# Self attention with ALiBi in a decoder layer: the place of the row sums' transposes, of the head maxima and of the output copy in each head, and norm scales computed on GpSimd

## What is computed

```python
x = _layernorm(x + _L0_attn_ref(x, ...))       # rotary q, k; alibi = min(j - i, 0) * slope * 8; no mask
x = _layernorm(x + _L0_xattn_ref(x, ctx, ...)) # cross attention on 1601 context rows
x = _layernorm(x + _L0_ffn_ref(x, ...))        # 8 experts, the best 2 of each row
# attention: w = softmax(q @ k.T * SCALE + alibi); out = w @ v;  _layernorm: (x - m) / sqrt(v + 1e-5)
```

## Time and profile before

| | us |
|---|---|
| median of 3 executions | 1904.31 (1903.47 to 1906.08) |
| the profiled execution | 1906.57 |
| its span | 1904.8 |
| PE busy | 1745.0 (92%) |
| DVE busy | 1390.0 (73%) |
| ACT busy | 1174.9 (62%) |
| POOL busy | 355.5 (19%) |

### The profile page before, as it was taken

One profiled execution on the slowest core, in us unless ns is written; L12 is line 12 of the kernel. 1 busy time (PEld: TensorE's weight loads), 2 busy tenths in 40 slices (PEclk: granted clock), 3 DMA queues, 4 the chain that ended last, 5 costly groups with the idle time before them and its releaser, 6 DMA issues.

```text
span 1904.8 us, 30266 instructions
## 1 busy us (share of the span) xinstructions
PE 1745.0 (92%) x10422; PEld 906.8 (48%) x10422; DVE 1390.0 (73%) x2786; ACT 1174.9 (62%) x2401; POOL 355.5 (19%) x577
## 2 busy tenths in 40 slices
PE   6989999999999999988799999999999877999993
PEld 3433333333333333325444444444444266999993
DVE  7587999999999999914699999999999053010113
ACT  1214777777777777785148777777787842333333
POOL 8120222242222222111000000000000003333331
PEclk9986999999999999999879999999999977999997
DMA  7232000000100000011203001001012126777773
GB/s 261 104 130 73 28 28 28 28 27 32 35 31 31 31 31 28 2 42 63 92 1 101 33 24 39 29 27 40 24 34 78 45 94 188 193 209 194 205 186 105
DMA packets 72880, 141.78 MB, mean 74 GB/s; under 512 B 14156, under 2 KB 47325, under 8 KB 70509
## 3 DMA queue, kind: packets, MB, share of 16 engines
q1 hardware_dynamic: 65018, 129.48, 20.6%
q0 software_dynamic: 7712, 10.37, 3.4%
HBM read 110.71 MB, written 28.45 MB: 73 GB/s over the span
## 4 chain that ended last, share of the span: by engine, by line
PE 73%; DVE 11%; ACT 7%; issue 4%; DMA 3%; SPq 1%; POOL 0%; POOLq 0%; ACTq 0%; DVEq 0%
PE banks L995 21%; PE banks L982 21%; PE banks L940 8%; PE banks L1187 7%; PE banks L1197 7%; ACT XT L1257 5%; PE banks L886 4%; DVE skip L1444 2%; ACT late L1257 2%; DVE wset L1444 2%; DVE CM L1440 2%; DMA oper<-qD 2%; PE banks L951 1%; PE banks L894 1%; DVE banks L1472 1%
## 5 line engine op out<-in xcount | busy, mean ns | idle before, releaser
L1257 ACT ACTIVATE XT<-banks 128x512 f32<-128x512 f32 x1240 | 658.3, 603 | 229.5 <-PE banks L982 160.4
L940 PE MATMUL banks<-oper 52*128 52x512 f32 (+1 forms) x2048 | 712.4, 441 | 32.0 <-DVE CM L1444 12.6
L982 PE MATMUL banks<-oper 54*128 54x512 f32 x1856 | 673.3, 451 | 28.6 <-POOL oper L755 10.5
L982 PEld LDWEIGHTS banks<-oper 54*128 54x128 f32 x1856 | 302.6, 186 | 514.0 <-ACT XT L1257 305.5
L1435 DVE TENSOR_REDUCE CM<-banks 128x1 f32<-128x402 f32 x1024 | 512.8, 566 | 21.1 <-PE banks L940 9.3
L940 PEld LDWEIGHTS banks<-oper 52*128 52x128 f32 x2048 | 347.8, 191 | 139.5 <-DVE CM L1444 63.6
L1257 ACT ACTIVATE late<-banks 128x512 f32<-128x512 f32 x616 | 328.3, 604 | 85.7 <-PE banks L982 71.3
L995 PE MATMUL banks<-XT,VS 128*32 128x512 f32 x2480 | 334.4, 611 | 6.8 <-ACT XT L1257 6.1
L1615 DVE TENSOR_TENSOR YB<-banks,b2E 128x256 f32<-128x256 f32 x39 | 16.5, 424 | 250.0 <-PE banks L1197 250.0
L1336 ACT ACTIVATE HID<-banks,b1E 128x128 f32<-128x128 f32 x312 | 85.1, 381 | 181.3 <-DMA b1E<-in_b1T_dram 169.4
L995 PE MATMUL banks<-late,VS 128*32 128x512 f32 x1232 | 164.9, 607 | 2.9 <-ACT late L1257 2.6
(11 more groups left out here) (205 smaller groups left out, 1393.8 us busy)
## 6 DMA issues: line engine op xcount, KB each, us to landing
W<-in_w1T_dram SPq DMA_DIRECT2D x39, 1024.0 KB
oper<-kD SPq DMA_DIRECT2D x32, 256.0 KB
W2R<-in_w2T_dram SPq DMA_DIRECT2D x8, 1024.0 KB, 7.9
oper<-kxD SPq DMA_DIRECT2D x32, 208.0 KB
b2E<-in_b_dram SPq DMA_DIRECT2D x39, 128.0 KB
qD<-parts SPq DMA_DIRECT2D x8, 512.0 KB, 2.7
kD<-parts SPq DMA_DIRECT2D x8, 512.0 KB, 2.7
oper<-kD SPq DMA_DIRECT2D x32, 128.0 KB
```

What stands on the lines that cost most here:

```text
L940: mm = pe.matmul(slot[:, n * QB:n * QB + ch], QO[64 * g:64 * g + M_ROWS, c2, col:col + P], KO[64 * g:64 * g + M_ROWS, c2, k0:k0 + ch], sta ...
L982: pe.matmul(bank, KO[64 * g:64 * g + S_ROWS, c, b * P:(b + 1) * P], QO[64 * g:64 * g + S_ROWS, c, q0:q0 + QB], start=True, stop=True).then ...
L1257: act.activation(PT[(c * plan.nu + u) % PRING], score_bank(plan, u, h, c), ACT.Exp).then_inc(A.exps, 1)
```

## The change

- `sequence` gives tile SUM_AT of self attention an order of its own, `S0 m S1 m m S2 m V0 S3 m`, and `ring_items` puts the sum first in that tile's list, so it comes ahead of the tile's two blocks on PE and on DVE. In the other tiles one m, that between V0 and S3, is gone; only the tile with the shift has a beat for it, and the shift now follows S3.
- On DVE the head maxima are made after the diagonal's bias of tile 11 and not before it.
- ACT copies the accumulator after the third exponential of a head and not after the fourth.
- The three norms' scales come from POOL, with a power of -0.5, and not from ACT's root and DVE's Newton step.

```diff
+        if self.causal and b == SUM_AT:
+            return "S0 m S1 m m S2 m V0 S3 m".split()
...
-            items.append(("sum", 0, 0, -1, None))
+            items.insert(0 if self.causal else len(items), ("sum", 0, 0, -1, None))
...
-SELF = Plan(TT, QB, True, False, 1, {2: "m S0 m S1 m S2 m V0 m S3"})
+SELF = Plan(TT, QB, True, False, 1, {2: "m S0 m S1 m S2 m V0 S3"})
...
+            def group_scales(call):
+                for g in range(NG):
+                    p, n = g % 2, call * NG + g
+                    pool.wait_ge(s_grp, GT4 * (n + 1))
+                    if n >= 2:
+                        pool.wait_ge(s_xn, GT4 * (n - 1))
+                    pool.tensor_scalar(varG[:, p, 0, :], aggG[:, p, :, 1], EPS, None, ALU.add).then_inc(s_gsd, 1)
+                    pool.tensor_scalar(varG[:, p, 1, :], aggG[:, p, :, 0], -1.0, None, ALU.mult).then_inc(s_gsd, 1)
+                    pool.wait_ge(s_gsd, 3 * n + 2)
+                    pool.tensor_tensor(varG[:, p, 4, :], varG[:, p, 0, :], inverse_root[:, :].to_broadcast([P, GT4]), ALU.pow).then_inc(s_gsd, 1)
+                    pool.wait_ge(s_gsd, 3 * (n + 1))
+                    pool.tensor_tensor(varG[:, p, 5, :], varG[:, p, 1, :], varG[:, p, 4, :], ALU.mult).then_inc(s_gsc, 1)
...
-                        if u == 3 and not first:
+                        if u == (2 if A is SA else 3) and not first:
                             save(h - 1)
...
-                    act.wait_ge(s_grp, call * NG + g + 1)
-                    act.activation(varG[:, p, 1, :], varG[:, p, 0, :], ACT.Sqrt).then_inc(s_gsd, 1)
...
+                        if b == plan.nb - LEAD and h + 2 < H:
+                            head_maxima(h + 1, pos + off - 1)
                         for item in plan.ring_items(b, h):
...
-                        link(dve.bn_aggr(aggG[:, p, q, :], statsG[:, q, :]), s_ln)
-                    dve.tensor_scalar(varG[:, p, 0, :], aggG[:, p, :, 1], EPS, None, ALU.add).then_inc(s_grp, 1)
-                    dve.wait_ge(s_gsd, call * NG + g + 1)
-                    link(dve.reciprocal(varG[:, p, 2, :], varG[:, p, 1, :]), s_ln)
...
+                        ins = dve.bn_aggr(aggG[:, p, q, :], statsG[:, q, :])
+                        ins.then_inc(s_grp, 1)
```

More of the change, by code:

```diff
@@ L217, in layer @@
         varG = sb("varG", [P, 2, 6, GT4])
+        inverse_root = sb("inverse_root", [P, 1])
         persistent, sb = sb, lambda name, shape, dt=F32: attention_memory.enter_context(nc.sbuf_tensor(name, shape, dt))
@@ L705, in _ @@
             pool.memset(zeros[:, :], 0.0)
+            pool.memset(inverse_root[:, :], -0.5)
             pool.wait_ge(s_zero, 2)
@@ L804, in _ @@
             pool.wait_ge(SA.pv, SELF.nb * H)
+            group_scales(0)
             attention(XA, CROSS, VX)
@@ L834, in _ @@
                       allow_small_or_imprecise_dtypes=True).then_inc(s_aux, 1)
+            group_scales(1)
             pool.wait_ge(s_same, 1)
@@ L867, in _ @@
                                             YS[:, i % 2, j, :], None, compute_op=ALU.add).then_inc(s_add, 16)
+            for g in range(TT // 4):
+                c = slice(4 * g, 4 * g + 4)
+                pool.wait_ge(s_varF, 4 * (g + 1))
+                pool.tensor_scalar(varF[:, 0, c], aggF[:, c, 1], EPS, None, ALU.add).then_inc(s_sdF, 1)
+                pool.tensor_scalar(varF[:, 1, c], aggF[:, c, 0], -1.0, None, ALU.mult).then_inc(s_sdF, 1)
+                pool.wait_ge(s_sdF, 3 * g + 2)
+                pool.tensor_tensor(varF[:, 4, c], varF[:, 0, c], inverse_root[:, :].to_broadcast([P, 4]), ALU.pow).then_inc(s_sdF, 1)
+                pool.wait_ge(s_sdF, 3 * (g + 1))
+                pool.tensor_tensor(varF[:, 5, c], varF[:, 1, c], varF[:, 4, c], ALU.mult).then_inc(s_nF, 1)
+                pool.wait_ge(s_nF, g + 1)
         @block.tensor
@@ L1341, in _ @@
             for g in range(TT // 4):
[L1342 to L1347, removed]
+                normalize(g)
         @block.vector
@@ L1421, in attention, with head_maxima @@
                 ch = plan.chunk
+                def head_maxima(h, pos):
+                    n = 2 * h
+                    dve.wait_ge(A.freed, pos + 1)
+                    dve.tensor_reduce(NM[:, :], CM[:, :, 0:2 * (3 - plan.beats)], AX.X, ALU.max, negate=True).then_inc(A.chain, 1)
+                    dve.wait_ge(A.chain, n + 1)
+                    dve.tensor_copy(SHW[:, 0:TT].bitcast(F32R), NM[:, :]).then_inc(A.chain, 1)
+                    dve.wait_ge(A.chain, n + 2)
+                    dve.tensor_tensor(SHW[:, TT:2 * TT].bitcast(F32R), NM[:, :], SHW[:, 0:TT], ALU.subtract).then_inc(A.cols, 1)
                 def ring_item(item, pos, bank, h, c):
@@ L1445, in ring_item @@
                                                      ALU.add, ALU.max, CM[:, a, b:b + 1]).then_inc(A.freed, 1)
[L1446 to L1454, removed]
                     elif kind == "shift":
@@ L1475, in step @@
                             off += 1
+                        if b == plan.nb - LEAD - 1 and h + 2 == H:
+                            head_maxima(h + 1, pos + off - 1)
                 pos = 0
@@ L1481, in attention @@
                     ring_item(item, pos, pos, -1, RING - 1)
+                    if item[4] == "last":
+                        head_maxima(0, pos)
                     if alibi:
```

25 lines of the change are left out of this document (4 added, 21 removed).

## The result

The changed kernel takes 1919.80 us (median of 5 executions, 1914.82 to 1945.19) where the kernel before took 1904.31: a ratio of 1.0065, 95% interval 1.0043 to 1.0087, so 12.4 us slower; the two medians lie 15.5 us apart, since the ratio leaves out the slow execution of 1945.19 us. A second set gave 1918.69 and 1.0061 (1.0040 to 1.0083). The forecast was 1910.1 with a range to 1920: slower as foreseen, and by the mechanism foreseen, but at least twice as much, and the median lies only 0.2 us inside the range.

A forecast was written before the change was run, and what follows sets the result against it. In self attention two loops of equal length, PE with ACT and DVE, leave DVE nothing to spare. Self attention +15.4 and norms -9.6 gave +5.8 on 1904.31: 1910.1 us, own range 1903 to 1918, outer 1888 to 1920.

The forecast's parts named there:

- The sum's place: Self attention, tiles 2 to 4: the early sum costs 1.3 us a head over 14 heads, copy's gain included.
- M2' behind V: Tile 2: the second block's second beat queues behind V on PE, leaving DVE idle 0.9 us before its second reduction.
- upper bound of 1.5: The sum's term a head, with exposed weight loads and the gap ahead of the transposes both in full.
- estimates for a drain: One more TensorE drain in tile 2: some 1.4 us more over the stage at the upper bound, some 3 less without drain.
- The copy: ACT's accumulator copy one exponential sooner, 15 heads: V of tile 1 gains 0.1 us at most, taken as -0.1.
- The shift and the head maxima: Tiles 11 and 12, 14 heads: S0 starts earlier, DVE's idle 0.58 shrinks by 0.2; -0.2 us a head.
- The norms: Three norms' scales on POOL: -2.3 us first, -1.8 second, -5.5 last; together -9.6, bounds -2 to -17.
- Last norm: Behind DVE's shorter statistics, POOL's 1.5 us and ACT's four end at 1896.9 instead of 1902.6: -5.5 us, -2 to -7.
- rival D: POOL's power takes 3 us or more, so POOL paces the last norm; +17, 1921 us; chance 0.08.
- Rival B: Same sum cost, but norms save 15 us as PE keeps its clock and POOL's steps are short; 1904.7; chance 0.18.
- Rival C: The early sum costs DVE nothing and tile 2 gains: -0.6 instead of +1.3 a head, 1883.5 us; chance 0.14.
- the replay: Tiles 2 to 4 worked through in the old profile's times: tile 2's bias at 301.35, DVE's second reduction at 304.85.

The follow-up runs named there:

- e2: The changed kernel with the second beat of tile 2's second block put ahead of V; 1909.13 us, ratio 1.0019 to the kernel before.
- e1: The kernel before with the sum's move in tile 2 alone, all else as it was; 1925.26 us, ratio 1.0099.
- e5: e3 with the head maxima back ahead of the bias of tile 11, the shift still behind S3; 1904.37 us, ratio 1.0002.
- e3: The changed kernel with the sum back last in tile 2 and the old order there; 1893.55 us, ratio 0.9935 to the kernel before.
- e7: e3 with the last norm's last group of scales from ACT's root and DVE's Newton step instead of POOL; 1895.78 us, ratio 0.9963.
- e9: e3 with the edits of both e5 and e7; 1897.26 us, ratio 0.9980 to the kernel before.
- e11: The kernel before with only the three norms' scales moved to POOL; 1898.67 us, ratio 0.9980.
- e4: The changed kernel run once more, unchanged; 1918.69 us, ratio 1.0061 to the kernel before.

## Why the prediction was right, and where it was off

**The sum's place, right in mechanism and in size.** The step said +1.3 a head with the copy's 0.1 in it; measured 1.41. It named DVE's waits in tile 2: about 0.35 for the transposes, 0.2 for the first block, 0.9 for M2' behind V; they are 0.29, 0.33 and 0.69. The first of these had luck in it: the 0.69 after which DVE "sees" the transposes was read at 303.27 to 303.96, where DVE was in a reduction until 304.00, so that row did not show how soon they are visible; the changed kernel, where DVE does wait, happens to give the same 0.69 (304.81 to 305.50). V of tile 2 to V of tile 3 is 3.71, "about 3.7". e2 shows that the headline, M2' behind V, is a good half of it (0.79), and that the two smaller waits ahead of it carry the other 0.62. Without the copy the term is 1.44 (e1) to 1.47, close to its upper bound of 1.5. The prediction's estimates for a drain took the upper bound of 1.5 without the copy, its range for self attention took it with the copy. The Trainium skill, TensorEngine Tiling, section Key Properties, says that a change of tiling mode drains TensorE. No run isolates a drain; e2, which keeps the transposes where they are, leaves room for it only inside those 0.62.

**The copy, right.** -0.06 of the -0.1 at most.

**The shift and the head maxima, wrong.** This is the step that failed: "the sum of bias, three small steps and two reductions is the same in both orders". The instructions are the same and their total is not: 0.52 us ahead of the bias, 0.61 behind it. The idle time before tile 12's bias shrank by 0.11 of the 0.2 forecast, and the order took 0.09 back. 14 x 0.2 = 2.8 us that never came. A good half of them, 14 x 0.12, was there to be had (e5).

**The norms, off in the parts and near in the sum.** First norm: -2.7 at the same clock (e1's 33.63 against 30.95) for -2.3. Second: -2.9 (36.14 against 33.23, the clock falling 28.3 and 27.7 us behind the copy) for -1.8, beyond its bound of -2.5; against e1, where it falls at 27.6, it is -3.6 (36.82 against 33.23). The working gave it the same waits on PE as the first norm and then a smaller gain for no reason that a row showed. The roots also cost ACT loads of its function table, 1.28 us each, seven in the profile before and two now; but they are not what was gained: in the second norm the load starts 5.81 us behind the copy, and PE turns its next heads at 8.40 with it and without it. Last norm: ACT's last row does come 5.8 us sooner (12.8 behind the first statistics instead of 18.5), for the 5.5 of the step. But the span ends only 2.9 sooner. The working's last sentence on it was "Stores follow ACT by 1.7 us in both", and so they do (1.8); the end of the program was no longer theirs, and POOL's closing drain stood in no term. This is the second step that failed, and the range was wide enough for it. I followed the chain of waits to its last row and did not ask which engines must be idle for the program to end, and how long each takes for that. POOL's chain takes 1.94 (238 + 227 + 1040 + 199 ns and three waits) instead of 1.5, a little above its bound of 1.8: the power, 1.04, costs over twice the dearer row, 0.40; rival D (3 us or more) is out. (D's 2.7 is also a little high: 1905 against 1902.6 is 2.4.)

**The sum of it.** By stages: 14 x 1.41 - 2.7 - 2.9 - 2.9 = +11.2, against 15.4 - 9.6 = +5.8. Of the 5.4 between, 2.8 are the shift, 1.5 the sum's term, 2.6 the last norm, that is POOL's drain, less 1.5 that the first two norms gave more. The ratios, 1.0065 and 1.0061, say 12.4 and 11.6. Rival B is out for the second norm at least: the clock is at 0.50 there with the new norms too. Rival C needed DVE's second reduction below 303.6 in the old times; it starts 3.55 us behind the bias of tile 2 (304.91 to 308.46), which from the replay's bias at 301.35 is 304.9, where the forecast had 304.85.

**Chances.** Slower by over 0.2% had 0.58, and that is what both sets say. The forecast's own range, 1903 to 1918, holds the lowest executions (1914.7) and misses the median by 2; the outer range, to 1920, holds it by 0.2, which is luck, since no term of it stood for the 4 to 6 us by which most executions lie above the lowest.

## What to carry to other kernels

Where two engines run without slack, an order that serves one item sooner is paid by what is queued behind it: before moving an item ahead, write down for each later item of the tile what it now stands behind, and add all the waits, the small ones too. Two orders of the same instructions need not take the same time on one engine; take the start-to-start distance of each pair of neighbours from the trace and not the sum of durations. When work moves to an engine that had been through long before the end, look at how long that engine takes to close: it may become the end of the program.

## What the runs showed of the hardware

- POOL's closing drain is recorded with 6.72 us, 0.2 behind the end of its last step (6.722 in the changed kernel, e3, e7, e9). In the kernel before it is recorded with 8.51 from 1876.2, and POOL's last scatter ran until 1878.0 within it, which leaves 6.7 again. The drains of PE, DVE and ACT end within 0.1 us of their last instruction (in the changed kernel at 1915.80, 1934.26 and 1938.45 for 1915.75, 1934.21 and 1938.41).
- A power on 128 x 4 takes POOL 1.04 us, five times a product of the same shape (0.20).
- DVE's 128 x 128 addition starts 0.09 us behind the start of a 128 x 16 step that lasts 0.17, where the reduction starts 0.19 behind it. Statistics' aggregations without a wait between them start 0.06 to 0.10 apart (four in 0.38), where linked ones started 0.22 apart.
- PE's clock can fall to half in the last head of self attention and stay there for 7 us (e5) to 63 us (the changed kernel), with the same engine loads before it (PE busy 10.10 and 10.14 of 12 us) as where it stays full. Four of the 13 profiles have it (changed, e5, e7, e11), with the new and the old attention; in mid-stage none has it. The last head is where PE has no blocks of maxima to make and is less busy, 28.41 of 35 us in e4 against 94.36 of 100 in mid-stage. What decides it is open.
